# Two zone stages and a second attention: each batch is normalised for the next stage, the last stage keeps its weights, the attention runs by slots

## The reference, cut to what matters

```
x = x + 0.5 * moe(layernorm(x))        # f0: 8 experts, top 2, and a shared one
x = x + gqa(layernorm(x))              # a0: 16 heads of width 8
x = x + 0.5 * moe(layernorm(x))        # f0
x = x + 0.5 * zones(layernorm(x))      # f1
x = x + mla(layernorm(x))              # a1: 8 heads of width 128 + 32 (rotary part)
x = x + 0.5 * zones(layernorm(x))      # f1, the same weights
return x

def layernorm(x): return (x - mean(x)) / sqrt(var(x) + 1e-5)     # per token

def zones(x):                          # D=128, D_FF=512, 8 zones, top 3, per BATCH
    h = tanh(mean_over_tokens(x) @ W1 + b1)
    p = softmax(h @ W2 + b2); top_p, top_i = top_k(p, 3); w = top_p / sum(top_p)
    return x + sum over the 3 zones e of batch b:  w[b,e] * (gelu(x[b] @ Wa[e]) @ Wb[e])

def mla(h):                            # latent attention, widths 32
    c_q, c_kv = h @ W_DQ + b_DQ, h @ W_DKV + b_DKV
    q = [c_q @ W_UQ + b_UQ, c_q @ W_QR + b_QR]      # 8 heads
    k = [c_kv @ W_UK + b_UK, h @ W_KR + b_KR];  v = c_kv @ W_UV + b_UV
    return softmax(q k^T / sqrt(160)) v, heads joined, @ W_O + b_O
```

## Time and profile before

| | us |
|---|---|
| three runs | 1702.57, 1706.13, 1710.29; median 1706.13 |
| the profiled execution | 1699.83 |
| its span (first to last record) | 1697.9 |
| PE busy | 1491.4 (88%) |
| DVE, ACT, POOL busy | 1101.3 (65%), 968.0 (57%), 561.2 (33%) |
| mean granted clock of PE | 0.933 of 2.4 GHz |

### The profile page before, as it was taken

One profiled execution on the slowest core, in us unless ns is written; L12 is line 12 of the kernel. 1 busy time (PEld: TensorE's weight loads), 2 busy tenths in 40 slices (PEclk: granted clock), 3 DMA queues, 4 the chain that ended last, 5 costly groups with the idle time before them and its releaser, 6 DMA issues.

```text
span 1697.9 us, 28196 instructions
## 1 busy us (share of the span) xinstructions
PE 1491.4 (88%) x9488; PEld 1192.8 (70%) x9488; DVE 1101.3 (65%) x2276; ACT 968.0 (57%) x1680; POOL 561.2 (33%) x478
## 2 busy tenths in 40 slices
PE   4799999779999999699999969998588888876998
PEld 4688888545555555578888857998466666656998
DVE  4666666688888886566666663666456666644665
ACT  5455554346666666454454554876345555555876
POOL 5355555500000000045555544675200000024675
PEclk9999999789999999599999967999579999977999
DMA  4000000000000000000000030000000000030000
GB/s 157 0 1 0 0 0 0 0 1 1 1 1 1 2 1 1 1 0 1 0 0 0 0 151 1 1 1 2 0 1 2 1 2 1 2 100 1 14 14 26
DMA packets 13748, 20.64 MB, mean 12 GB/s; under 512 B 720, under 2 KB 8912, under 8 KB 13392
## 3 DMA queue, kind: packets, MB, share of 16 engines
q1 hardware_dynamic: 13648, 19.31, 3.3%
HBM read 17.21 MB, written 2.10 MB: 11 GB/s over the span
## 4 chain that ended last, share of the span: by engine, by line
PE 68%; issue 10%; DVE 10%; ACT 9%; POOL 2%; DMA 1%; DVEq 0%; SPq 0%; POOLq 0%; ACTq 0%
PE PS L546 14%; PE PS L1520 8%; PE PS L1533 8%; PE PS L573 8%; PE PS L701 3%; PE PS L680 2%; PE PS L688 2%; ACT AR L793 2%; PE PS L564 2%; PE PS L658 2%; PE PS L367 1%; DVE AR L1201 1%; PE PS L1012 1%; POOL RR L481 1%; PE PS L1026 1%
## 5 line engine op out<-in xcount | busy, mean ns | idle before, releaser
L481 POOL TENSOR_TENSOR RR<-AR,RR 128x512 fp32r<-128x512 f32 x224 | 289.5, 1292 | 632.3 <-ACT RR L505 632.3
L519 ACT ACTIVATE AR<-PS 128x512 f32<-128x512 f32 x224 | 134.0, 598 | 237.3 <-PE PS L546 236.7
L459 DVE TENSOR_TENSOR AR<-AR,PS 128x512 f32<-128x512 f32 x224 | 153.9, 687 | 145.5 <-PE PS L546 129.3
L793 ACT ACTIVATE AR<-PS 128x512 f32<-128x512 f32 x256 | 149.6, 600 | 99.2 <-PE PS L688 97.8
L862 DVE TENSOR_REDUCE AR<-PS 128x2 f32<-128x512 f32 x256 | 173.5, 686 | 49.5 <-PE PS L680 47.6
L573 PE MATMUL PS<-RR,WD 128*128 128x512 f32 x672 | 193.4, 396 | 4.5 <-POOL RR L481 4.2
L463 DVE TENSOR_TENSOR AR<-AR,PS 128x512 f32<-128x512 f32 x224 | 154.1, 688 | 35.9 <-DVE AR L459 31.4
L546 PE MATMUL PS<-XHI,WG 128*128 (+1 forms) x448 | 176.1, 393 | 0.0
L546 PE MATMUL PS<-XHI,WU 128*128 (+1 forms) x448 | 174.7, 390 | 0.0
L1520 PE MATMUL PS<-XHI,SL 128*128 128x256 f32 x768 | 159.9, 291 | 9.0 <-DVE XTR L1640 6.1
L573 PEld LDWEIGHTS PS<-RR,WD 128*128 128x128 f32 x672 | 123.3, 188 | 40.6 <-POOL RR L481 16.7
(11 more groups left out here) (273 smaller groups left out, 3303.3 us busy)
## 6 DMA issues: line engine op xcount, KB each, us to landing
RAWZ<-in_zone_up SPq DMA_DIRECT2D x16, 256.0 KB, 4.5
RAWZ<-in_zone_down SPq DMA_DIRECT2D x16, 256.0 KB, 4.9
AR<-in_w SPq DMA_DIRECT2D x1, 2688.0 KB, 13.9
X<-in_x SPq DMA_DIRECT2D x4, 512.0 KB, 6.4
out_x<-X SPq DMA_DIRECT2D x4, 512.0 KB, 3.2
XT<-in_w SPq DMA_DIRECT2D x1, 1608.0 KB, 9.0
XT<-in_sel SPq DMA_DIRECT2D x1, 896.0 KB, 12.2
SM<-in_small SPq DMA_DIRECT2D x1, 857.5 KB, 6.8
```

The source lines that it names most:

```text
L459: v.tensor_tensor(PRD[:, m % 2, :], SIL[:, m % 2, :], bank(2 + m % 2), ALU.mult).then_inc(S.prod, 1)
L481: g.tensor_tensor(HL[:, m % 2, :], GAT[:, m % 2, :], HH[:, m % 2, :].bitcast(F32), ALU.subtract).then_inc(S.h_lo, 1)
L519: act.activation(SIL[:, m % 2, :], bank(m % 2), ACT.Silu).then_inc(S.silu, 1)
L793: act.activation(PT[:, g % 2, k, 2 * jp:2 * jp + 2, :], bank(2 + m % 2).rearrange("p (j q) -> p j q", j=2), ACT.Exp, scale=SC0).then_inc(S ...
```

## The change

Three things, and what they need.

**1. Each batch is normalised for the stage behind it** in the first `f1` and in `a1` (`early(n)`). After `add(b)`, DVE takes `bn_stats` and then `bn_aggr` (mean and variance in one). POOL adds epsilon, raises to the power -0.5 (`POWER`), and normalises the two tiles into `XNB` (`next_normed`, four instructions). PE transposes them (`next_turn`) and DVE, or ACT in `a1`, copies them into `XF`, the normalised and turned `x`, at a place of its own. ACT's copy in `a1` also sums the columns for the router. The common normalisation of `a1` and of the last `f1` goes. In the last `f1`, `early_high` and `early_low` make the rounded and low parts from `XF`, the second half of them inside the loop (`late_low`).

**2. The zone weights stay in `ZW`** for the last stage: its 16 transfers, 8 roundings and 8 low parts go. `a1` no longer uses `WTS` and `XHI` for its tiles, but `XTR`, `RR` and a part of `AR`. Splitting the prepared weights moves into the router phase of the first `f1`.

**3. `a1` is ordered by slots.** A step has 8 slots `m`; slot `m` has `S` number `3 + m` counted on from batch `i + 1` and `T` number `m` of batch `i`. Head keys come in four quarters with a bank each (two in slot 3, two in slot 5), `maxima(i + 1)` in slot 6.

The core of the diff:

```diff
+        def next_stats(v, n, b, stat):
+            ch = Chain(v, N.chain, links.get("next", 0))
+            for i in range(TPB):
+                last = v.bn_stats(stat[:, i, :], X[:, b * TPB + i, :])
+            ch.link(last)
+            for i in range(TPB):
+                last = v.bn_aggr(MV[:, b * TPB + i, :], stat[:, i, :])
+            last.then_inc(N.ln, 1)
...
+        def next_normed(g, n, b):
+            g.wait_ge(N.ln, normed_before(n) + b + 1)
+            ts = slice(b * TPB, (b + 1) * TPB)
+            g.tensor_scalar(LN[:, 5, ts], MV[:, ts, 1], EPS, None, ALU.add).then_inc(N.var, 1)
+            g.wait_ge(N.var, normed_before(n) + b + 1)
+            g.tensor_tensor(RSTD[:, ts], LN[:, 5, ts], POWER.to_broadcast([P, TPB]), ALU.pow).then_inc(N.rstd, 1)
+            g.wait_ge(N.rstd, normed_before(n) + b + 1)
+            wait(g, N.tr, b, turned_before(n))
+            for t in range(TPB):
+                k = slice(b * TPB + t, b * TPB + t + 1)
+                last = g.tensor_scalar(XNB[:, t:t + 1, :], X[:, k, :], MV[:, k, 0], RSTD[:, k], ALU.subtract, ALU.mult)
+            last.then_inc(N.xn, 1)
...
@@ a1_pool @@
+            g.memset(KXL1[64:P, :].bitcast(F32), 0.0).then_inc(S.blank, 1)
+            g.wait_ge(S.blank, 5)
+            for at in ONE_AT:
+                g.memset(KXL1[at:at + 1, :].bitcast(F32), 1.0).then_inc(S.blank, 1)
...
@@ a1_pe @@
             def maxima(b):
                 pe.wait_ge(S.mm, b + 1)
-                wait(pe, S.kp_lo, 2 * (b + 2) if b + 2 <= NB else 2 * NB)
+                wait(pe, S.kp_lo, NQ1 * (b + 1) + 3 if b + 1 < NB else NQ1 * NB)
...
             def step(i):
+                now, next_, far, done, gone = (0 <= i + d < NB for d in (0, 1, 2, -1, -2))
+                for m in range(NS1):
+                    b, s = divmod(NS1 * (i + 1) + LEAD1 + m, NS1)
+                    if m == 3 and far:
+                        head_keys(i + 2, 0)
+                        head_keys(i + 2, 1)
+                    if m == 5 and far:
+                        head_keys(i + 2, 2)
+                        head_keys(i + 2, 3)
+                    if 0 <= b < NB:
+                        scores(b, s)
                     if now:
                         scores_t(i, m)
+                    if m == 0 and far:
+                        project(i + 2)
+                    if m == 1 and done:
+                        values(i - 1, 1)
+                    if m == 3 and gone:
+                        next_turn(i - 2)
+                    if m == 3 and done:
+                        turn(i - 1, 1)
+                    if m == 5 and now:
                         values(i, 0)
+                    if m == 5 and done:
+                        back(i - 1)
+                    if m == 6 and next_:
+                        maxima(i + 1)
+                    if m == 7 and now:
                         turn(i, 0)
+                    if m == 7 and done:
+                        project_out(i - 1)
...
@@ a1_act, step: behind exps(i, m) of the slot @@
+                    if m == 4 and far:
+                        head_keys(i + 2, 0)
+                        head_keys(i + 2, 1)
...
+                    if m == 6 and far:
+                        head_keys(i + 2, 2)
+                        head_keys(i + 2, 3)
...
@@ a1_dve, step: behind smax(b, s) of the slot @@
+                    if m == 4 and next_:
+                        maxima(i + 1)
+                    if m == 4 and done:
+                        normalise(i - 1, 1)
+                    if m == 4 and far:
+                        head_keys(i + 2, 0)
+                        head_keys(i + 2, 1)
+                    if m == 6 and far:
+                        head_keys(i + 2, 2)
+                        head_keys(i + 2, 3)
...
@@ f1_pe, the loop over z @@
                 if z % TOP1 == 2 and z > TOP1:
                     back(z // TOP1 - 1)
+                if early(n) and z % TOP1 == 2 and z > 2 * TOP1:
+                    next_turn(z // TOP1 - 2)
...
@@ f1_pool @@
-            def select(b):
+            def select(b, behind):
                 for k in range(TOP1):
-                    e = g.value_load(IDX[0:1, bass.ds(b * TOP1 + k, 1)], min_val=0, max_val=E1 - 1)
+                    if behind and k == 1:
+                        next_normed(g, n, b - 3)
+                    e = g.value_load(IDX[0:1, b * TOP1 + k:b * TOP1 + k + 1], min_val=0, max_val=E1 - 1)
...
+            for b in range(NB):
+                select(b, early(n) and b > 2)
```

More of the change, by code:

```diff
@@ L1020, in values @@
                     wait(pe, S.ao, 2 * b - 1)
+                    wait(pe, N.xt, b - 1, turned_before(n))
                 else:
@@ L1052, in project_out, with next_turn @@
                 last.then_inc(S.out, 1)
[L1054 to L1072 removed]
+            def next_turn(b):
+                pe.wait_ge(N.xn, normed_before(n) + b + 1)
+                if b + 1 < NB:
+                    pe.wait_ge(S.ao, 2 * (b + 1) + 1)
+                for t in range(TPB):
+                    last = pe.transpose(bank(6)[:, t * P:(t + 1) * P], XNB[:, t, :], ident)
+                last.then_inc(N.tr, 1)
@@ L1542, in back, with next_turn @@
                 last.then_inc(S.back, 1)
+            def next_turn(b):
+                pe.wait_ge(N.xn, normed_before(n) + b + 1)
+                for t in range(TPB):
+                    last = pe.transpose(bank(6 + b % 2)[:, SEQ + t * P:SEQ + (t + 1) * P], XNB[:, t, :], ident)
+                last.then_inc(N.tr, 1)
             for z in range(NZ):
@@ L1556, in f1_act @@
             act = nc.scalar
-            f1_norm_act(n)
+            if not (n and early(n - 1)):
+                f1_norm_act(n)
             act.wait_ge(S.r_pe, D.r_pe + 1)
@@ L1563, in f1_act @@
                 prep_act(n + 1)
+            if n and early(n - 1):
+                for c in range(4, NC):
+                    early_high(n, c)
             act.wait_ge(S.idx, D.idx + 1)
@@ L1705, in _ @@
             for n, kind in enumerate(stages):
-                if kind == "f1":
+                if kind == "f1" and not early(n - 1):
                     f1_sp(n)
```

425 lines of the change are left out of this document (224 added, 201 removed).

## The result

The changed kernel took 1797.5 us (median of 4 runs, 1791.2 to 1800.6). The kernel before took 1706.1 (median of its three fast runs; a fourth, at 1790.5 us, was a slow one and is left out). The ratio is 1.053, 95% interval 1.048 to 1.058. It is slower, as forecast, by 91 us where 57 were forecast. The profiled execution took 1794.6 us, with a span of 1792.8 against 1697.9.

The account below looks back on a forecast made before the run. PE was taken to bound the two loops, chains over several engines the stretches between. Terms summed to +22.5 us at full clock, plus 35 for the clock: +57.5 on 1699.83, stated as 1760 us; range 1732 to 1790, 8 in 10: 1712 to 1806.

Parts of the forecast that it names:

- (A): `a1`, slot 5: PE waits 2.5 us from last issue for the low part of key quarter 2.
- (B): `a1`, slot 6: PE's `maxima` waits 2.1 us from last issue, behind ACT's rounding and DVE's low part.
- (C): `a1`, slot 3: PE waits 1.3 us before key quarter 0, for ACT's `inputs` and DVE's `low_inputs`.
- the seams: Stretches between loops: into `a1` -18 us (-16 to -19), into the last `f1` -24 us (-20 to -25).
- below 0.95: Sign: the granted clock of both loops, first zone stage and `a1`, falls below 0.95 if the forecast holds.
- The mis-sized term: First `f1` loop: PE waits 2.25 us for POOL's normalising in batches 0 to 12, +29.3 us (25 to 43).
- half a fall: First zone stage: each of 13 waits costs 0.75 us more through a lower clock, +10 us (0 to 20).
- the tail: End of `a1`: no waits for quarters in the last two steps, one transposition added, -2 us (-5 to +2).
- Rival 4: Clock falls in every long wait and returns late, in `a1` and the zone stage: 1808 to 1814 us, chance 0.12.
- Rival 1: Clock doesn't fall in gaps of 2 us, all else holds: +22.5 us, 1722 to 1728, chance 0.15.
- Rival 2: `a1` slots work, PE never waits, step 13.5 us, zone waits stay: -51 us, 1649 to 1655, chance 0.13.
- The router phase: First `f1` before its zone matmuls: two more ACT copies and two DVE low parts, +1 us (0 to +5).

Follow-up runs that it names:

- `norm_first`: Changed kernel with POOL's `next_normed` put ahead of its wait for `down` in the first zone stage, instead of behind the copy: 1753.8 us.
- `a1_plain`: Changed kernel where `a1` keeps only `bn_stats` for the last stage, which normalises, loads and splits its weights itself: 1819.3 us.
- `both_tuned`: Changed kernel with POOL normalising a pair earlier, `a1` reordered on TensorE, ScalarE and VectorE, and three further order moves: 1630.7 us, ratio 0.958 to the kernel before.
- `a1_pe`: Changed kernel, TensorE's order in `a1` alone: transposed scores and `values` ahead of key quarters 2 and 3, maxima moved to slot 7: 1772.1 us.

## Why the prediction was right, and where its sizes were off

**The sign and the mechanisms held.** TensorE waits in front of L1625 and in the three places (A), (B) and (C); the seams shrink by 40 us and the loops grow by more. The size did not hold as well: 1797.5 us lies outside the forecast's own range (1732 to 1790) and inside the wider one for 8 in 10. Of the signs named beforehand, the waits, the periods and the seams came, and the granted clock of the zone loop fell to 0.87; in the 14 full steps of `a1` it only went from 0.98 to 0.95, so the sign "below 0.95" failed there by a little.

**The mis-sized term is `next_normed`.** I took 1.05 us for POOL's four instructions, "nearest to the small copies", with bounds of 0.8 and 2.1. They took 2.8, above the upper bound. The bound compared with an addition of 512 columns and divided by four, 0.32 us for each tile; a tile took 0.83. The power (721 ns for two columns) stayed within the 1.28 us that this bound gave it. Against the 1.05 itself, the two tiles took 1.65 instead of 0.6 and the power 0.72 instead of 0.2. So the wait, by the periods, is 4.03 us and not 2.25: 13 x 1.78 = 23 us too little. By the prediction's estimate from the Trainium skill, "GPSIMD Engine Reference", section 4.1 (about line rate with one input, some 0.15 us each), it would have been further off still; the trace has 0.83 and the measurement decides. The prediction also says that no row has an instruction with one input, but POOL's cast in the earlier trace rows is one: 1.04 us for 1024 columns, 1.0 ns a column, where L248 takes 6.5 ns a column.

**The clock in the zone loop** is the second half: I took half a fall a batch, 0.75 us, and it fell each time, 1.76: 13 x 1.0 = 13 us. The two make 36 us of the 36 by which that loop's forecast fell short (78.8 against 43). It is one mistake more than two, since here the clock fell more often behind the longer wait: with waits of 1.83 us, `norm_first` had a fall in 5 of 12 batches, which at 1.5 us each is 0.6 a batch, close to the 0.75 forecast for a wait of about 2 us.

**Second attention.** That +51.3 came out near +55.4 is in part luck. The 14 full steps grew by 54 us (234.0 to 288.1) where 41 + 25 = 66 were forecast. In them, the step at full clock was forecast at 19.5 and is 20.03: 14 x 0.5 = +7. The clock was forecast at 1.8 us a step and costs 1.3 in every third: 14 x 1.4 = -19. The start shrank by 6.7 us (forecast 8.6), and the tail grew by 4.0 (30.3 to 34.3) where it was to shrink by 2, so these two are 8 us the other way; by `a1_plain` most of the tail's growth comes with the normalising. The 0.5 a step is not in (A), (B) and (C), whose sum of 6.0 us was good: 20.03 less the 14.25 of a step without waits is 5.8. It is in the waits of the kernel before, which I put at 3.3 us counted from issue; by the same 14.25 us they were 16.54 + 0.25 - 14.25 = 2.5. Rival 4 (every long wait falls, from the Trainium skill, "TensorE: Matmul & The Clock Gate", section "HAM oscillation") holds for the waits of 3.81 us in the zone stage and not for the pair of 2.28 and 2.05 us in `a1`, where two steps of three have no fall. Rival 1 (no falls in gaps of 2 us) is refuted by the other third: behind the wait of 2.28 us at 1456.44 the clock was 0.56 up to 1459.50. The falls in the zone stage say nothing about it, since the waits there were longer than its 2 us.

**Rival 2** described what could be: I put the `a1` step without waits at 13.5 us, and 17.15 as the step below which it wins. The order in the changed kernel doesn't get there; `both_tuned`, with the same work, does at 14.25.

**The router phase** was forecast at +1 and shows +4.5. But the first zone matmul lies between 1036.3 and 1045.2 in the traces of the 11 experiments, whose program up to there is that of the changed kernel. So 4.5 us between single profiles can't be told from nothing.

**Open.** Why the clock fell in every third step of `a1`, in every second of `a1_plain`, whose waits are the same, and in none of `a1_pe` read here, with waits of 1.81, 1.15 and 1.88 us, was not tried.

## What to carry to other kernels

Normalising each batch for the next stage, with the split moved and the weights kept, shortened the two seams by 40 us. The work itself cost some 4 us in each of the two stages: 153.1 against 149.3 in the zone loop, once POOL, which had time to spare, did it one pair before TensorE asked, and 350.3 against 346.7 in `a1`. The rest of the loss was order. So when work is added to an engine that is "only busy 60%", ask what stands in front of it in that engine's queue, and whether that itself waits for the engine which will need the answer. Price an instruction that the trace lacks with a bound that also covers its form: a power of two columns took 0.72 us, and a tile with two operations in one instruction took 0.83 where a quarter of a 512 column addition is 0.32. And look at both sides of a hand-over: TensorE's order alone gave 25 us and that of the other two engines 55, both gave 80, and only with a further move on either side was TensorE busy throughout.
